# Adding expert rows into the output by accumulating DMA, in place of a gathered copy z, its read back and a last sum

## The reference

```
x = x + tanh(g_xattn) * attention(layernorm(x), ctx)
h = layernorm(x)                                        # 2048 tokens of 512
shared = (sigmoid(h @ sg.T) * (h @ su.T)) @ sd.T
weights = softmax(h @ router.T)                         # 8 experts, the best 2 are used
routed = sum over the 2 chosen experts e of  weight_e * ((sigmoid(h @ wg_e.T) * (h @ wu_e.T)) @ wd_e.T)   # bf16
out = x + tanh(g_ffn) * (h + shared + routed)
```

## Time and profile before

| | us |
|---|---|
| median of 3 runs | 331.34 (331.22 to 332.74) |
| the profiled execution, its own time | 332.47 |
| its span | 330.7 |
| PE busy, DVE busy, GpSimd busy in the span | 295.4, 216.4, 158.8 |

### The profile page before, as it was taken

One profiled execution on the slowest core, in us unless ns is written; L12 is line 12 of the kernel. 1 busy time (PEld: TensorE's weight loads), 2 busy tenths in 40 slices (PEclk: granted clock), 3 DMA queues, 4 the chain that ended last, 5 costly groups with the idle time before them and its releaser, 6 DMA issues.

```text
span 330.7 us, 6138 instructions
## 1 busy us (share of the span) xinstructions
PE 295.4 (89%) x1596; PEld 208.7 (63%) x1608; DVE 216.4 (65%) x585; ACT 132.0 (40%) x235; POOL 158.8 (48%) x238
## 2 busy tenths in 40 slices
PE   7579789999999999999999998799999999997280
PEld 2247658786878776877887786566666666663120
DVE  0788878478756588745467488576777676775291
ACT  2263577606657406678104370134343434342000
POOL 3706892685701757402767046035565555565100
PEclk9999989999999999999999999999999999999587
DMA  7999699022060120000159994333434334339499
GB/s 247 342 229 319 98 210 291 27 96 79 20 237 0 50 80 0 0 4 0 64 116 210 208 207 154 83 89 121 124 100 110 113 97 126 98 99 314 134 316 343
DMA packets 30612, 45.91 MB, mean 139 GB/s; under 512 B 3008, under 2 KB 20160, under 8 KB 30592
## 3 DMA queue, kind: packets, MB, share of 16 engines
q1 hardware_dynamic: 20016, 27.66, 27.5%
q0 software_dynamic: 10432, 17.99, 22.9%
q10 hardware_dynamic: 144, 0.00, 0.0%
HBM read 39.58 MB, written 14.72 MB: 164 GB/s over the span
## 4 chain that ended last, share of the span: by engine, by line
PE 68%; DMA 7%; DVE 7%; POOL 7%; issue 6%; ACT 2%; SPq 1%; POOLq 0%; DVEq 0%; ACTq 0%
PE bank L677 13%; PE bank L472 11%; PE bank L473 11%; PE bank L474 11%; PE bank L694 7%; POOL xg L398 5%; PE bank L484 4%; PE bank L467 4%; PE bank L669 3%; PE bank L685 2%; DMA z<-ysb,desti 2%; DMA zb<-z 2%; DMA wqk_sb<-wqk 1%; DVE acc L1272 1%; DVE prob L951 1%
## 5 line engine op out<-in xcount | busy, mean ns | idle before, releaser
L888 ACT ACTIVATE sigc<-bank 128x352 f32<-128x352 f32 x39 | 18.1, 463 | 67.0 <-PE bank L677 67.0
L451 POOL DMA_INDIRECT z<-ysb,desti x36 | 36.1, 1002 | 9.6 <-issue 9.3
L472 PE MATMUL bank<-lnT_hi,sgu_lo 128*128 128x512 f32 (+2 forms) x96 | 39.1, 407 | 1.6 <-DVE lnT_lo L988 1.6
L473 PE MATMUL bank<-lnT_lo,sgu_hi 128*128 128x512 f32 (+2 forms) x96 | 37.8, 394 | 0.0
L474 PE MATMUL bank<-lnT_hi,sgu_hi 128*128 128x512 f32 (+2 forms) x96 | 37.8, 394 | 0.0
L398 POOL DMA_INDIRECT xg<-lnb,slot x32 | 31.9, 996 | 9.9 <-issue 7.6
L1239 DVE TENSOR_TENSOR hrow<-sigc,bank 128x352 bf16<-128x352 f32 x39 | 20.3, 521 | 24.3 <-ACT sigc L888 16.9
L677 PE MATMUL bank<-wgu_lo,xTb 128*128 x156 | 36.0, 313 | 0.0
L677 PE MATMUL bank<-wgu_hi,xTb 128*128 x156 | 36.0, 312 | 0.0
L387 POOL TENSOR_TENSOR hT_lo<-sig,hT_hi 128x512 fp32r<-128x512 f32 (+1 forms) x9 | 11.6, 1289 | 45.7 <-ACT hT_hi L800 45.7
L1245 DVE TENSOR_SCALAR ysb<-bank,wt 128x512 bf16<-128x512 f32 x39 | 29.1, 747 | 5.7 <-DMA z<-ysb,desti 2.8
(11 more groups left out here) (178 smaller groups left out, 651.1 us busy)
## 6 DMA issues: line engine op xcount, KB each, us to landing
xt<-xg SPq DMA_DIRECT2D x39, 129.0 KB
xT_raw<-xT SPq DMA_DIRECT2D x4, 1024.0 KB, 7.3
acc<-x SPq DMA_DIRECT2D x4, 1024.0 KB, 9.5
out<-acc SPq DMA_DIRECT2D x16, 256.0 KB, 3.5
wgu_lo<-wguT POOLq DMA_DIRECT2D x2, 1408.0 KB, 13.3
wgu_hi<-wguT POOLq DMA_DIRECT2D x2, 1408.0 KB, 13.3
cx<-ctxT SPq DMA_DIRECT2D x4, 512.0 KB, 4.3
wd_sb<-wdT POOLq DMA_DIRECT2D x2, 1024.0 KB
```

The lines of the kernel that those rows point to most:

```text
L451: nc.gpsimd.indirect_dma_start(out=z, out_offset=bass.IndirectOffsetOnAxis(ap=desti[:, r:r + 1], axis=0), in_=ysb[:, r, :], in_offset=None ...
L472: pe.matmul(dst, a_lo, b_hi, start=first, stop=False)
L473: pe.matmul(dst, a_hi, b_lo, start=False, stop=False)
L888: act.activation(sigc[:, v, :], bank[2 * v][:, 0:I], ACT.Sigmoid).then_inc(s["csig"], 1)
```

## The change

The expert rows are no longer written to z. `acc` tiles are stored to `out` as soon as the shared expert is in them (the base), between SP's loads. Out has 512 spare rows behind the 2048, written with zeros early (`dumped`, eight DMAs of 128 KB), for rows of a tile that belong to no token. `ysb` becomes fp32 with the same four slots, and each send is an indirect DMA that adds its 128 rows of 2 KB to rows of out in HBM (`compute_op=ALU.add`). z, za, zb, the identity matmuls, the last DVE sums and the stores at the end are gone. The first send waits for all 16 base stores (`outd`).

Two sends may not add to one row at the same time. Rows of one expert are different tokens, so tiles of one expert may overlap in flight, but the first tile of an expert may only be sent when all tiles ahead of it have landed. DVE makes a table with 16 at each first tile (`tables_firsts`), and SP, behind each `load_tile(v + 8)`, runs `release(v)`: it waits for landings and then counts `go`, for which GpSimd's send waits. For a first tile it waits for tiles v - 1 to v - 3, otherwise for tiles v - 5 and earlier. In the first two rounds part of the thresholds are constants: in round 0 every tile of it, and in round 1 every slot of the round before, so that tiles 1 to 4 each wait for the tile just ahead of them, and tile 5 does as an expert's first.

```diff
-    z = nc.dram_tensor("z", (TOP * TOK + NE * P, N), BF16, kind="Internal").ap()
...
+        (ysb,), y_end = place((("ysb", [P, SLOTS, N], F32),), sig_end)
...
+            for r in range(SLOTS):
+                sp.dma_start(out[TOK + r * P:TOK + (r + 1) * P, 0:N // 2], padr[:, 0:N // 2].bitcast(F32)).then_inc(s["dumped"], 16)
+                sp.dma_start(out[TOK + r * P:TOK + (r + 1) * P, N // 2:N], padr[:, 0:N // 2].bitcast(F32)).then_inc(s["dumped"], 16)
             for e in range(E + 1):
                 sp.dma_start(xg[e * REG:e * REG + P, :], padr[:]).then_inc(s["padout"], 16)
+            def store(t):
+                sp.wait_ge(s["shared"], t + 1)
+                sp.dma_start(out[t * P:(t + 1) * P, :], acc[:, t, :]).then_inc(s["outd"], 16)
...
+                if b > 1:
+                    for j in range(LT):
+                        store(LT * (b - 2) + j)
+            for j in range(LT):
+                store(LT * (last_b - 1) + j)
...
+            def release(u, r, q, ids):
+
+                known = isinstance(u, int)
+                for k in range(1, SLOTS):
+                    if r >= k:
+                        sp.wait_ge(s_yd[r - k], 16 if known and q == 0 else 16 * q + ids[r])
+                sp.sem_inc(s["same_round"], 1)
+                for k in range(1, SLOTS):
+                    if r < k and not (known and q == 0):
+                        sp.wait_ge(s_yd[r - k + SLOTS], 16 if known and q == 1 else 16 * (q - 1) + ids[r])
+                sp.sem_inc(s["go"], 1)
+
+            def firsts(q):
+
+                w = sp.value_load(first_i[0:1, bass.ds(q, 1)], min_val=0, max_val=FIRST ** SLOTS - 1)
+                return [(w // FIRST ** i) % FIRST for i in range(SLOTS)]
+
             for r in range(SLOTS):
                 load_tile(r, r, None)
-            with sp.Fori(1, QN) as q:
+            for j in range(LT):
+                store(LT * last_b + j)
+            for r in range(SLOTS):
+                load_tile(SLOTS + r, r, r + 1)
+            sp.wait_ge(s["firsts"], 1)
+            for q in range(2):
+                ids = firsts(q)
+                for r in range(SLOTS):
+                    load_tile(SLOTS * (q + 2) + r, r, SLOTS * (q + 1) + r + 1)
+                    release(SLOTS * q + r, r, q, ids)
+            with sp.Fori(4, QN) as q:
+                ids = firsts(q - 2)
                 for r in range(SLOTS):
                     load_tile(SLOTS * q + r, r, SLOTS * q + r - SLOTS + 1)
-            for u in range(SLOTS * QN, NE):
-                load_tile(u, u % SLOTS, u - SLOTS + 1)
-
-            zt = z[0:TOP * TOK, :].rearrange("(c t p) n -> c p t n", c=TOP, p=P)
-
-
-            sp.wait_ge(s["sent"], 1)
-            sent = [sp.value_load(sent_i[0:1, r:r + 1], min_val=16, max_val=16 * len(range(r, NE, SLOTS))) for r in range(SLOTS)]
-            for r in range(SLOTS):
-                sp.wait_ge(s_yd[r], sent[r])
-            for i in range(0, TT, LT):
-                sp.dma_start(za[:, i:i + LT], zt[0, :, i:i + LT]).then_inc(s["za_in"], 16)
-            sp.wait_ge(s["dm"], TT)
+                    release(SLOTS * (q - 2) + r, r, q - 2, ids)
+            for u in range(SLOTS * QN, NE + 2 * SLOTS):
+                if u < NE:
+                    load_tile(u, u % SLOTS, u - SLOTS + 1)
+                v = u - 2 * SLOTS
+                if v % SLOTS == 0:
+                    ids = firsts(v // SLOTS)
+                release(v, v % SLOTS, v // SLOTS, ids)
+
             for r in range(SLOTS):
                 sp.wait_ge(s_yd[r], 16 * len(range(r, NE, SLOTS)))
-
-            def store(t):
-                sp.wait_ge(s["comb"], t + 1)
-                sp.dma_start(out[t * P:(t + 1) * P, :], acc[:, t, :]).then_inc(s["outd"], 16)
-            for t in range(TT):
-                if t >= ZS:
-                    store(t - ZS)
-                sp.dma_start(zb[:, t % ZS], zt[1, :, t]).then_inc(s_zl[t % ZS], 16)
-            for t in range(TT - ZS, TT):
-                store(t)
-            sp.wait_ge(s["outd"], 16 * TT)
...
-            def send(u, r, q):
+            def send(u, r):
                 pool.wait_ge(s["yev"], u + 1)
-                if q is not None:
-                    pool.wait_ge(s_yd[r], 16 * q)
                 if isinstance(u, int) and u >= SLOTS * QN:
+                    pool.wait_ge(s["go"], u + 1)
                     nc.gpsimd.indirect_dma_start(
-                        out=z, out_offset=bass.IndirectOffsetOnAxis(ap=dest[:, u:u + 1], axis=0),
-                        in_=ysb[:, r, :], in_offset=None).then_inc(s_yd[r], 16)
+                        out=out, out_offset=bass.IndirectOffsetOnAxis(ap=dest[:, u:u + 1], axis=0),
+                        in_=ysb[:, r, :], in_offset=None, compute_op=ALU.add).then_inc(s_yd[r], 16)
                     return
                 nc.gpsimd.tensor_copy(desti[:, r:r + 1], dest[:, bass.ds(u, 1)]).then_inc(s["didx"], 1)
                 pool.wait_ge(s["didx"], u + 1)
+                pool.wait_ge(s["go"], u + 1)
 
                 nc.gpsimd.tensor_tensor(carrier[:], half[:], half[:], ALU.add)
                 nc.gpsimd.indirect_dma_start(
-                    out=z, out_offset=bass.IndirectOffsetOnAxis(ap=desti[:, r:r + 1], axis=0),
-                    in_=ysb[:, r, :], in_offset=None).then_inc(s_yd[r], 16)
-
+                    out=out, out_offset=bass.IndirectOffsetOnAxis(ap=desti[:, r:r + 1], axis=0),
+                    in_=ysb[:, r, :], in_offset=None, compute_op=ALU.add).then_inc(s_yd[r], 16)
+
+            pool.wait_ge(s["dumped"], 16 * 2 * SLOTS)
+            pool.wait_ge(s["outd"], 16 * TT)
             for r in range(SLOTS):
-                send(r, r, None)
+                send(r, r)
             with pool.Fori(1, QN) as q:
                 for r in range(SLOTS):
-                    send(SLOTS * q + r, r, q)
+                    send(SLOTS * q + r, r)
             for u in range(SLOTS * QN, NE):
-                send(u, u % SLOTS, QN)
+                send(u, u % SLOTS)
...
-                    link(V.tensor_tensor(second[:, c, :], rank_of[:, c, :], rank_of[:, 1 - c, :], ALU.is_lt))
-                    V.scalar_tensor_tensor(out=lnb[c][:, :, DST], in0=second[:, c, :], scalar=float(TOK),
-                                           in1=token[:, LT * b:LT * (b + 1)], op0=ALU.mult, op1=ALU.add).then_inc(s["order"], 1)
+                    V.tensor_copy(lnb[c][:, :, DST], token[:, LT * b:LT * (b + 1)]).then_inc(s["order"], 1)
...
+            def tables_firsts():
+
+                flat = is_first[:].rearrange("p q r -> p (q r)")
+                link(V.memset(flat, 0.0))
+                link(V.tensor_tensor(big2[:], start, across(ntile), ALU.mult))
+                link(V.tensor_reduce(over[:], big2[:], AX.X, ALU.add))
+                link(V.tensor_tensor(flat[:, 0:NE], over[:], tile_no[:, 0:NE], ALU.is_equal))
+                link(V.tensor_tensor(first_digits[:], is_first[:], first_at[:].rearrange("p (a i) -> p a i", a=1)
+                                     .to_broadcast([P, NQ, SLOTS]), ALU.mult))
+                link(V.tensor_reduce(first_pack[:], first_digits[:], AX.X, ALU.add))
+                V.tensor_copy(first_i[:], first_pack[:]).then_inc(s["firsts"], 1)
...
-            pe.wait_ge(s["yev"], NE)
-            pe.wait_ge(s["za_in"], 16 * NB)
-            for t in range(TT):
-                pe.wait_ge(s_zl[t % ZS], 16 * (t // ZS + 1))
-                at_least(pe, s["comb"], t - 3)
-                pe.matmul(bank[t % 4][:, :], identb[:], za[:, t, :], start=True, stop=False)
-                pe.matmul(bank[t % 4][:, :], identb[:], zb[:, t % ZS, :], start=False, stop=True).then_inc(s["zsum"], 1)
...
-            for t in range(TT):
-                dve.wait_ge(s["zsum"], t + 1)
-                V.tensor_tensor(acc[:, t, :], bank[t % 4][:, :], acc[:, t, :], ALU.add).then_inc(s["comb"], 1)
```

More of the change, by code:

```diff
@@ L34 @@
 TOP = 2
+SLOTS = 4
+SPARE = SLOTS * P
 def at_least(eng, sem, n):
@@ L63, in gated_block @@
     last_b = NB - 1
+    FIRST = 32
     HOT = 9
@@ L131, in gated_block @@
         powers = sb("powers", [P, 2 * SLOTS - 1])
+        first_at = sb("first_at", [P, SLOTS])
         epack_i = sb("epack_i", [P, NQ], U32)
@@ L1226, in _ @@
             shared_out(last_b, 2)
-            tables_sent()
+            tables_firsts()
             def rows_out(u, r):
```

41 lines of the change are left out of this document (17 added, 24 removed).

## The result

| | before | after |
|---|---|---|
| median | 331.30 (331.22 to 332.74, 4 runs) | 362.25 (360.25 to 363.38, 4 runs) |
| ratio to before | | 1.0916, 95% interval 1.086 to 1.0973 |
| span of the profiled execution | 330.7 | 361.6 |

The forecast was 325.3 us with a range of 315 to 341: it is wrong in sign and size. The kernel went the way of the second rival, in which the landings eat more than the tail was worth, and 19 us beyond the price worked out for it. In all tables the time is the median of all executions, and the ratio leaves out those over 1.5% above the fastest of their kernel.

What follows compares the result with a forecast made beforehand. PE was taken to bound the expert loop, with a 24 us tail behind the last result. 18.2 us gained and 12.2 given back by ordered sends made -6.0 us, so 325.3 us, range 315 to 341.

Steps and rivals of the forecast that it cites:

- the second rival: Landing chain of the sends eats more than the tail: at L = 5.0 the end is 342.1, 343 us; chance 0.35.
- start of tile 0's send: First send on GpSimd: xev at 218.38 + 0.3 + 1.15 + 0.4 + 0.44 = 220.7.
- 12 steps that wait for a landing: Sends of tiles 1 to 5 and later first tiles: each starts L + 0.65, 4.55 us, after the one ahead.
- L: Time from GpSimd's start of an accumulating send to its landing: 3.9 us, bounds 2.7 and 6.86.
- GpSimd's send "taken as unchanged": GpSimd's instruction for 128 descriptors stays 1.00 us; anything more would be added to L.
- the 0.3 us to the end: End of the span: 0.3 us from the last send's landing to the end.
- SP's 1.8 us per tile: Between waits, SP's load, release and table reading set the recovery pace: 1.6 to 1.95 us per tile, taken as 1.8.
- The forecast's list of what would prove it wrong: L outside 3.5 to 4.3, DMA_INDIRECT much over 1.00, SP's pace above 2.2, or first tile load later than 207.82.
- They fill to 82%, but do not bound: DMA engines in the expert stage: 30.8 of 37.8 engine-us per tile, at 42 ns per KB and 512 KB.
- the 0.8 that I had as the worst: Load of tile 4 behind the last four base stores: at worst 0.8 us late, taken as 0.3.
- the 312.5 of the sum with sends as free as before: End if sends were as free as before, following from tile 36's result at about 302.6; would save 18.2 us.
- The bound of L at 6.86: Upper bound of L, from a send that shared its engines with a heavy read.

Runs made afterwards that it cites:

- the window of three: Changed kernel, but every send waits only for the landing three tiles earlier, first tiles for nothing more: 325.34 us, ratio 0.9799 to before.
- The padded run: Changed kernel's order with overwriting sends, plus three more small GpSimd additions ahead of each send of tiles 0 to 35: 338.96 us, against 329.08 unpadded.
- later runs: The window of three, 325.34 us, and the same with two base stores issued before SP's wait for the scatter, 325.55 us.
- a window of two: Changed kernel, but each send waits only for the landing two tiles earlier: 343.74 us, ratio 1.0316 to before.
- its overwriting twin: The window of three with sends that overwrite rows of out and add nothing: 319.91 us, ratio 0.9615 to before.

## Why the prediction was wrong

The forecast's sum can be laid beside the trace term by term. The 39 starts of sends in POOL's timeline give the measured column.

| term | forecast | measured | difference |
|---|---|---|---|
| start of tile 0's send | 220.7 | 222.16 | +1.5 |
| 12 steps that wait for a landing (tiles 1 to 5, 10, 15, 19, 24, 28, 32, 37) | 54.3 | 72.6 | +18.3 |
| the 26 other steps | 45.5 | 58.9 | +13.4 |
| start of the last send to the end | 4.2 | 7.96 | +3.75 |
| end of the span | 324.7 | 361.6 | +36.9 |

**The mechanism** was right as far as the order goes. The waits stand where the forecast put them, sends of first tiles come late, DVE waits for landings, PE behind it, and the last landings stand behind tile 36 in a row. Taking the waits away (the window of three) gives back 37 us. The failure is in sizes. Two steps of the forecast make most of it: **L, "which no row shows"**, put at 3.9 and measured at 5.1, and **GpSimd's send "taken as unchanged"**, 1.57 us and not 1.00. The third, smaller one is the 0.3 us to the end.

**L.** I built 3.9 from a bf16 landing of 2.6, 1.0 for a second operand and 0.3 for HBM. Measured are 4.5 at the least and 5.1 in the median, and a step that waits is 6.05 on average and not 4.55. The base was nearly right: overwriting fp32 rows land in 2.9. The addition was wrong twice. I priced the add at twice the bytes, while an adding send takes 2.5 times the engine time of an overwriting one. And I took GpSimd's instruction as unchanged with the promise that more would be added to L; its 0.57 is in L by measurement. Together, (114 - 46) x 0.25 MB / 16 = 1.1 us more on each engine and 0.57 on GpSimd, with the 2.7 to 2.9 of overwriting sends, make an estimate of 4.4 to 4.6: the quiet landing. Longer ones come behind sends that follow one another at 2.2 us: the steps to tiles 10 and 15 were 7.15 and 6.76 us, and that to tile 5, behind sends far apart, 5.43. With tiles 1 to 4 sent close together it became 7.00. That such sends share the engines is the likely reason, not one that a run takes apart.

The Trainium skill (DMA: Bandwidth & Descriptors, Anatomy of one DMA) fits 2.0 us plus bytes / 436e3 to a GpSimd DMA, from which 3.2 us was an estimate with the bytes of both operands counted. The adding sends of this trace do not agree: it is short by 1.3 at the least, and the measurement decides.

**GpSimd's pace.** SP's 1.8 us per tile was to set the recovery between waits, with GpSimd's minimum of 1.71 below it. GpSimd's instruction is 1.57, its minimum 2.20, and 26 steps came to 2.26 on average. Next to PE's 2.36 that leaves nothing with which to catch up. The padded run shows this cost apart: 8.8 us for 0.42 us per send. The forecast's list of what would prove it wrong named "a DMA_INDIRECT much longer than 1.00" and a pace above 2.2; the first came, and the pace came too, 2.26, though GpSimd set it and not SP. Neither had a price in the rivals beyond what was promised to L. That is why the rival of 343 us, at L = 5.0, is still 19 us short.

**The DMA engines.** "They fill to 82%, but do not bound" used 42 ns per KB and 512 KB. At PE's pace they are at 0.97 (window of three), and in the changed kernel at 0.65 with over a third fewer matmuls. The rate was fit for overwriting sends (46 us of engine time per MB in the view above, so 46 ns per KB), and wrong for adding ones (114). What this step cost the changed kernel is within L; that full engines bound anything more is not shown.

**The end.** I gave 0.3 us from the last landing to the end. It is 3.4 (353.65 + 4.6 for the landing, 361.6). No row shows what fills it. It stands in overwriting kernels too, whose spans end 7.5 us behind the start of the last send. The kernel with no sends ends 3.8 us behind its last result, so as much stands there without any send. Before, the span ended about with the landing of the last store (started at 327.2, with 3.5 us to land in the median), 6.8 us behind DVE's last sum (323.93); that the stores covered such a time is argued.

**The start.** Of 1.5 us, 1.4 is in SP's queue: the load of tile 8, behind which tile 0 is released, ends at 221.20, where the sum had 219.8 (218.38 + 0.3 + 1.15). SP's timeline in the changed kernel, and below it DVE's results of tiles 0 and 1:

```profile
208.25 4.12 SPq L273 DMA_DIRECT2D xt<-xg  x4
212.42 2.03 SPq L248 DMA_DIRECT2D out<-acc  x4
215.77 7.46 SPq L273 DMA_DIRECT2D xt<-xg  x6
```

```profile
217.54 0.75 DVE L1268 TENSOR_SCALAR ysb<-bank,wt 128x512 f32<-128x512 f32 x1
...
220.94 0.75 DVE L1268 TENSOR_SCALAR ysb<-bank,wt 128x512 f32<-128x512 f32 x1 [0.29 <-PE bank L721]
```

The four stores take 2.0 us of SP where its next load would have been, and tile 4's load comes 3.35 us later than that place, far more than the 0.8 that I had as the worst. The loads of tiles 5 to 8 follow close behind it. The second result stands 3.4 us behind the first, which is PE's 2.36 for a tile and 1.0 more. That later runs cover it with a slower first tile leaves its price at the end of the span open.

**The gain** was less than forecast. The kernel whose sends overwrite in a window of three ends at 319.0 and not at the 312.5 of the sum with sends as free as before, and the floor with no sends at all ends at 310.9. Tile 36's send starts at 308.95 and not 302.8. Of these 6.1 us, 3.4 are there at the first send (224.1 against 220.7) and 2.7 come behind it. The sum's wait for a landing ahead of tile 37, which this window does not have, gives 3.0 back, and the end behind the last send takes 7.5 us where I had 4.2.

**Chances.** 0.35 for slower was not far off in kind, but the high end of the range, 341, came from L alone. The bound of L at 6.86 was known, and each 0.1 was worth 1.3 us (above 3.9 even 1.6, by the rival's own sum: 324.7 to 342.1 for 1.1). With L's measured 5.1 the sum would still have said some 344 us; the range missed since the terms beside L had no upper ends.

## What to carry to other kernels

An accumulating indirect DMA removes a read back and its sums, and puts its landing into a chain wherever two sends may meet in one row of the output: count the sends that must wait, times the landing of an adding send (4.5 to 5.1 us here for 128 rows of 2 KB), before counting the tail that goes. Keep several in flight where the rows allow it; a window of three, which is right only for inputs like this one, made the same change 2% faster than before, a window of two 3% slower, and a strict order at 12 places 9% slower. Before forecasting an operation that no trace shows, price each engine that it touches apart (issuer, DMA engines, landing, program end) and give each its own upper end.

## What the runs showed of the hardware

- Adding 128 rows of 2 KB takes GpSimd 1.57 us against 1.00 for overwriting them; adding 64 rows still takes 1.44.
- The same bytes take 2.5 times the DMA engines' time when added, in nearly twice as many packets (2303 for 4.20 MB against 1299 for 4.27 MB), and the bytes in the profile do not count the side that is read: HBM read and written are the same 35.38 and 20.88 MB on the pages of the adding kernel and of its overwriting twin.
- The landing of an adding send goes with its rows: 3.8 us for 64, 5.1 for 128 in the same order. An overwriting send of 128 rows of 2 KB lands in 2.9, and one of 1 KB in 2.8.
- A program whose last instruction is a send from GpSimd ended 7.5 us behind its start when it overwrote, and 7.9 to 9.2 us when it added. With no send at all the span ended 3.8 us behind the last result.
